# One more edge tile per turn by TensorE instead of GpSimd's gather, in each of two graph layers

## The reference

```python
h = jnp.maximum(_layernorm(x), 0.0)
# first layer
hw = h @ W0 + b0
agg = segment_sum(edge_weight[:, None] * hw[src], dst)
deg = segment_sum(edge_weight, dst)
x = x + relu(agg / (deg[:, None] + 1e-06))
h = jnp.maximum(_layernorm(x), 0.0)
# second layer
msg = gelu(concatenate([h[src], edge_attr]) @ W_msg + b_msg)
agg = segment_sum(msg, dst)
out = x + gelu(((1 + eps) * h + agg) @ W_upd + b_upd)
```

## Time and profile before

| | |
|---|---|
| median of 3 runs | 3535.41 us (3535.20 to 3536.32) |
| the profiled execution | 3536.93 us, span 3535.1 us |
| mean granted TensorE clock | 0.907 of full |
| PE, PEld busy | 82%, 78% of the span |
| POOL busy | 73%, 2,570.7 us |
| DVE, ACT busy | 61%, 55% |
| indirect DMAs (tiles gathered) | 1,323 in the first layer, 1,372 in the second |
| DMA engines | mean 62 GB/s |

### The profile page before, as it was taken

One profiled execution on the slowest core, in us unless ns is written; L12 is line 12 of the kernel. 1 busy time (PEld: TensorE's weight loads), 2 busy tenths in 40 slices (PEclk: granted clock), 3 DMA queues, 4 the chain that ended last, 5 costly groups with the idle time before them and its releaser, 6 DMA issues.

```text
span 3535.1 us, 89327 instructions
## 1 busy us (share of the span) xinstructions
PE 2887.9 (82%) x31003; PEld 2758.6 (78%) x31004; DVE 2160.5 (61%) x3525; ACT 1944.3 (55%) x6492; POOL 2570.7 (73%) x2720
## 2 busy tenths in 40 slices
PE   1988888887888888888778888888888888888887
PEld 1987877877877777778777878787787878787877
DVE  5766666666666666666655555556565655565653
ACT  3655565655555656555565555555454555555553
POOL 4777777777777777777457777777777777777774
PEclk9999999999899899999678989898988899898988
DMA  3322222222222222222123333333333333333331
GB/s 97 60 48 53 50 48 50 50 52 50 48 53 50 48 50 50 52 50 48 32 63 74 75 73 77 74 81 72 76 74 74 74 74 74 74 74 74 74 74 48
DMA packets 277341, 220.23 MB, mean 62 GB/s; under 512 B 81018, under 2 KB 208518, under 8 KB 277314
## 3 DMA queue, kind: packets, MB, share of 16 engines
q0 software_dynamic: 86240, 88.48, 16.6%
q1 hardware_dynamic: 191074, 131.40, 13.1%
HBM read 214.39 MB, written 5.30 MB: 62 GB/s over the span
## 4 chain that ended last, share of the span: by engine, by line
POOL 71%; issue 24%; SPq 2%; PE 1%; POOLq 1%; DMA 1%; ACT 1%; DVE 0%; DVEq 0%
POOL rows L436 71%; PE ps L719 1%; SPq L307 1%; SPq L328 0%; POOLq L434 0%; ACT sums_sb L566 0%; DMA h_table<-h_sb 0%; POOLq L427 0%; SPq L300 0%; DMA p_table<-h_sb 0%; PE ps L745 0%; PE ps L679 0%; DMA rows<-h_table,idx 0%; SPq L304 0%; DVE h_sb L834 0%
## 5 line engine op out<-in xcount | busy, mean ns | idle before, releaser
L647 PE MATMUL ps<-parts,pick_all 125*128 125x192 bf16 x19600 | 1767.9, 253 | 54.6 <-DVE pick_all L930 30.8
L930 DVE TENSOR_SCALAR pick_all<-src_bc,node_f 125x1280 bf16<-125x1280 int16 (+1 forms) x1960 | 1740.0, 953 | 71.1 <-issue 52.7
L647 PEld LDWEIGHTS ps<-parts,pick_all 125*128 125x128 bf16 x19600 | 1692.6, 101 | 87.5 <-issue 57.1
L436 POOL DMA_INDIRECT rows<-p_table,idx x1372 | 1295.6, 944 | 440.0 <-issue 440.0
L436 POOL DMA_INDIRECT rows<-h_table,idx x1323 | 1248.6, 944 | 415.9 <-issue 415.9
L511 ACT ACTIVATE onehot<-iota,dw 128x72 f32<-128x72 f32 x3136 | 809.3, 342 | 0.0
L679 PE MATMUL ps<-onehot,room 128*65 128x72 f32 (+1 forms) x6272 | 546.4, 248 | 268.9 <-ACT room L541 262.5
L679 PEld LDWEIGHTS ps<-onehot,room 128*65 128x65 f32 (+1 forms) x6272 | 488.4, 155 | 328.1 <-ACT room L541 293.5
L586 ACT ACTIVATE room<-room 128x512 f32<-128x512 f32 x196 | 123.6, 630 | 783.9 <-DVE room L1095 783.3
L1095 DVE TENSOR_TENSOR room<-ps,rows 128x512 f32<-128x512 f32 x196 | 135.5, 691 | 618.0 <-DMA rows<-p_table,idx 600.7
L769 PE MATMUL ps<-W1b_sb,eT 128*128 128x128 f32 x1568 | 259.7, 318 | 252.1 <-ACT eT L581 251.9
(11 more groups left out here) (87 smaller groups left out, 567.2 us busy)
## 6 DMA issues: line engine op xcount, KB each, us to landing
src_bc<-last_src SPq DMA_DIRECT2D x196, 312.5 KB
ea<-in_edge_attr_dram SPq DMA_DIRECT2D x196, 256.0 KB, 5.4
rows<-p_table,idx POOLq DMA_INDIRECT x1372
rows<-h_table,idx POOLq DMA_INDIRECT x1323
src_bc<-last_src SPq DMA_DIRECT2D x49, 156.2 KB
x_sb<-in_x_dram SPq DMA_DIRECT2D x5, 312.5 KB
h_table<-h_sb SPq DMA_DIRECT2D x5, 312.5 KB
p_table<-h_sb SPq DMA_DIRECT2D x5, 312.5 KB
```

The source lines that it names most:

```text
L436: nc.gpsimd.indirect_dma_start(out=rows[:, s, j, 0:D], out_offset=None, in_=table[:, :], in_offset=bass.IndirectOffsetOnAxis(ap=idx[:, s, ...
L647: last = nc.tensor.matmul(psG[(s + shift) % 2], pick[layer][(s + shift) // 2 % 2][0:PN, n, at:at + P], parts[:, n, :], start=(n == 0), sto ...
L930: last = nc.vector.tensor_scalar(pick[layer][i][0:PN, c * KN:(c + 1) * KN, :], src_bc[:, i, :, 0:w], node_f[:, c:c + 1], None, ALU.is_equal)
```

## The change

The extra tiles move from slot 2 of the first layer to the odd slots: 1 and 3 in the first layer (two for each body instead of one), and 1 in the second (one instead of none). `JP` becomes [7, 6, 7, 6] and [7, 6, 7, 7]. Three pairs in four (counted over the two layers) have a pick of three tiles now. The 50 matmuls of an extra tile are done in two halves of 25: the first half after the `gather` of the even group before it, the second before the `gather` of its own group.

In the second layer TensorE's `edge_product` of g+1 comes behind `windows` of g.

The table with target and weight numbers side by side (`dw_tab`, fp32) is split into `dst_tab` (int16) and `w_tab` (fp32); ScalarE copies both for a group in the first layer, and the target numbers alone in the second. Some one-time rows of the preparation now lie in the room of the pick buffer.

```diff
-    EXTRA = 2
-    JP = [[JG - (layer == 0 and s == EXTRA) for s in range(SLOTS)] for layer in range(2)]
+    EXTRA = ((1, 1), (1, 0))
+    JP = [[JG - (s % 2 == 1 and EXTRA[layer][s // 2]) for s in range(SLOTS)] for layer in range(2)]
...
-        dw_tab = sb("dw_tab", [P, NG, 2, J])
+        dst_tab = sb("dst_tab", [P, NG * J], i16)
+        w_tab = sb("w_tab", [P, NG * J])
...
+        def width(layer, i):
+            return PE3 if EXTRA[layer][i] else PE2
+        def extras(layer, b, i):
+            return b * sum(EXTRA[layer]) + sum(EXTRA[layer][0:i + 1])
...
# SyncE, load_bc
-                if layer == 0 and i == 0:
+                if EXTRA[layer][i]:
...
# ScalarE
-                nc.scalar.copy(dw[:, slot, :, :].rearrange("p q j -> p (q j)"),
-                               dw_tab[:, bass.ds(g, 1), :, :].rearrange("p a q j -> p (a q j)")).then_inc(s_dw[layer], 1)
+                if layer == 0:
+                    nc.scalar.copy(dw[:, slot, 1, :], w_tab[:, bass.ds(g * J, J)])
+                nc.scalar.copy(dw[:, slot, 0, :], dst_tab[:, bass.ds(g * J, J)]).then_inc(s_dw[layer], 1)
...
-                    if s == EXTRA:
-                        act.wait_ge(s_xrow, b + 1)
+                    if s % 2 and EXTRA[0][s // 2]:
+                        act.wait_ge(s_xrow[0], extras(0, b, s // 2))
...
# TensorE
+            def extra(layer, i, half):
+                for n in range(half * NK // 2, (half + 1) * NK // 2):
+                    last = nc.tensor.matmul(psX, pick[layer][i][0:PN, n, PE2:PE3], parts[:, n, :],
                                             start=(n == 0), stop=(n == NK - 1))
                 return last
+            def next_gathers(layer, b, s):
+                i = (s + 1) // 2 % 2
+                if s % 2:
+                    gather(layer, b, s, 1)
+                    if EXTRA[layer][i]:
+                        pe.wait_ge(s_xrow[layer], extras(layer, b + (s + 1) // SLOTS, i) - 1)
+                        extra(layer, i, 0)
+                else:
+                    if EXTRA[layer][i]:
+                        extra(layer, i, 1).then_inc(s_xpicked[layer], 1)
+                    gather(layer, b, s, 1)
...
             def second(b, last_body):
                 for s in range(SLOTS):
                     if not (last_body and s == SLOTS - 1):
                         edge_transpose(b, s, 1)
-                        gather(1, b, s, 1)
-                        edge_product(b, s, 1)
+                        next_gathers(1, b, s)
                     pe.wait_ge(s_msg, b * SLOTS + (s + 1 + 2))
                     windows(1, b, s, lambda j, s=s: msg[:, s % 2, j * D:(j + 1) * D], D)
+                    if not (last_body and s == SLOTS - 1):
+                        edge_product(b, s, 1)
...
# VectorE: the base of each group is taken off dst_tab (int16 in and out), padding is -20000
+            def extra_rows(layer, b, s):
+                dve.wait_ge(s_xpicked[layer], extras(layer, b, s // 2))
+                nc.vector.tensor_reduce(rows[:, s + 1, JG - 1, 0:D], psX.rearrange("p (q d) -> p d q", q=SPLIT),
+                                        AX.X, ALU.add).then_inc(s_xrow[layer], 1)
...
                     if not (last_body and s == SLOTS - 1):
+                        if s % 2 == 0 and EXTRA[1][s // 2]:
+                            extra_rows(1, b, s)
                         picked_rows(1, b, s, 1)
                         message_sum(b, s, 1)
```

More of the change, by code:

```diff
@@ L133, in two_layer_gnn @@
         src_bc = sb("src_bc", [PN, 2, KN, PE3 + 16], i16)
-        pick_all = sb("pick_all", [P, NK * (PE3 + PE2)], bf16)
-        pick = [[pick_all[:, 0:NK * w].rearrange("p (n e) -> p n e", n=NK),
-                 pick_all[:, NK * PE3:NK * (PE3 + PE2)].rearrange("p (n e) -> p n e", n=NK)] for w in (PE3, PE2)]
+        pick_all = sb("pick_all", [P, 2 * NK * PE3], bf16)
+        pick = [[pick_all[:, i * NK * PE3:i * NK * PE3 + NK * (PE3 if EXTRA[layer][i] else PE2)].rearrange(
+            "p (n e) -> p n e", n=NK) for i in range(2)] for layer in range(2)]
         flat_f = pick_all[:, :].bitcast(fp32)
@@ L496, in _ @@
                 high(0, u)
-            take(2, dw_tab[:, :, 0, :].rearrange("p g j -> p j g"), s_dwt)
+            take(2, dst_tab[:, :].rearrange("p (g j) -> p j g", j=J), s_dwt)
             for u in range(UNITS):
                 middle(0, u)
-            take(4, dw_tab[:, :, 1, :].rearrange("p g j -> p j g"), s_dwt)
+            take(4, w_tab[:, :].rearrange("p (g j) -> p j g", j=J), s_dwt)
             act.wait_ge(s_tables, 1)
@@ L649, in gather @@
                 last.then_inc(s_picked[layer], 1)
-            def extra(q):
-                for n in range(q * NK // 4, (q + 1) * NK // 4):
-                    last = nc.tensor.matmul(psX, pick[0][0][0:PN, n, PE2:PE3], parts[:, n, :],
+            def extra(layer, i, half):
+                for n in range(half * NK // 2, (half + 1) * NK // 2):
+                    last = nc.tensor.matmul(psX, pick[layer][i][0:PN, n, PE2:PE3], parts[:, n, :],
                                             start=(n == 0), stop=(n == NK - 1))
                 return last
[L658 to L669, removed]
+            def next_gathers(layer, b, s):
[9 more added lines that the diff above has]
+                    gather(layer, b, s, 1)
             def windows(layer, b, s, lhs, width):
@@ L694, in _ @@
             gather(0, 0, 0, 0)
-            extra(0)
-            extra(1).then_inc(s_xused, 1)
+            if EXTRA[0][0]:
+                extra(0, 0, 0)
             pe.wait_ge(s_tables, 1)
@@ L701, in first @@
                     if not (last_body and s == SLOTS - 1):
-                        gather(0, b, s, 1)
-                    next_extra(b, s, last_body)
+                        next_gathers(0, b, s)
                     pe.wait_ge(s_used[s], b + 2)
@@ L776, in _ @@
             gather(1, 0, 0, 0)
+            if EXTRA[1][0]:
+                extra(1, 0, 0)
             edge_product(0, 0, 0)
@@ L915, in onehots @@
                                         ALU.is_equal).then_inc(done, 1)
-            def width(layer, i):
-                return PE3 if layer == 0 and i == 0 else PE2
             def sources(layer, i, turn):
@@ L942, in next_pick @@
                     dve.wait_ge(s_pick[layer], 2 * b + (s + 3) // 2)
-                    if layer == 0 and s == 1:
-                        dve.wait_ge(s_xused, b + 1)
                     sources(layer, (s + 3) // 2 % 2, b + ((s + 3) // 4 + 1))
-                    last = pick_half(layer, (s + 3) // 2 % 2, 0)
-                    if layer == 0 and s == 1:
-                        last.then_inc(s_half, 1)
+                    pick_half(layer, (s + 3) // 2 % 2, 0)
                 else:
@@ L1021, in first @@
                     if not (last_body and s == SLOTS - 1):
+                        if s % 2 == 0 and EXTRA[0][s // 2]:
+                            extra_rows(0, b, s)
                         picked_rows(0, b, s, 1)
-                        if s == 1:
-                            extra_rows(b)
                     if last_body and s == 1:
@@ L1091, in message_sum @@
                 dve.wait_ge(s_em, g + 1)
-                dve.wait_ge(s_gat[slot], BODIES * 16 * JP[0][slot] + (b + (s + shift) // SLOTS + 1) * (16 * JG))
+                dve.wait_ge(s_gat[slot], BODIES * 16 * JP[0][slot] + (b + (s + shift) // SLOTS + 1) * (16 * JP[1][slot]))
                 dve.wait_ge(s_prow[1], g + 2)
+                if slot % 2 and EXTRA[1][slot // 2]:
+                    dve.wait_ge(s_xrow[1], extras(1, b, slot // 2))
                 dve.wait_ge(s_msg, g + 1)
```

25 lines of the change are left out of this document (10 added, 15 removed).

## The result

| | before | after |
|---|---|---|
| median | 3535.60 us (3535.20 to 3536.32, 4 runs) | 3414.22 us (3412.40 to 3414.84, 4 runs) |
| profiled execution, its span | 3536.9 us, 3535.1 us | 3412.4 us, 3410.6 us |
| granted clock, mean | 0.907 | 0.97 |
| first gather to last, first layer | 1650.5 us | 1590.2 us |
| last gather of the first to first of the second | 69.0 us | 67.5 us |

The ratio is 0.9653, 95% interval 0.9640 to 0.9667. The forecast was 3415, range 3406 to 3440. The two layers gave 60.4 and 61.3 us, the step between them 1.5 and the start 1.3 (first gather at 66.8 instead of 68.1 us).

What follows compares the result with a forecast made beforehand. GpSimd's number of gathers was taken as the bound, TensorE next. Profiled 3536.9 - 122.3 for gathers + 1.4 for layer ends = 3416.0; that execution being 1.5 us above the median, 3414.5, say 3415 us; range 3406 to 3440.

Steps and rivals of the forecast that it cites:

- Gathers: GpSimd, both layers: one gather fewer in each of 49 bodies, 61.1 and 61.2 us, together 122.3 us saved.
- TensorE's full-clock body: TensorE with the extra tile, without waits: 29.8 us against 32.4 in the first layer, 31.1 against 33.7 in the second.
- The slow-clock loss shrinks: TensorE's lower-clock work after waits: falls to 1 or 2 us a body, mean clock from 0.91 to 0.95 or more.
- Rival A: TensorE, both layers: lower clock after waits makes bodies 35.9 and 37.2 us; about 3756 us, 3459 with half the loss; 5%.
- The hand-over of the pick "just fits": VectorE to TensorE, second layer: pick ready some 6.6 us after the edge product, wanted 6.76 + 0.5 us after it.
- Rival B: Second layer: TensorE and VectorE hold each other up, 34.4 us a body instead of 33.7, +34 us, 3449 us; 8%.
- The order of the edge product costs and brings nothing: TensorE, second layer, edge product behind the one-hot product: between 1.2 us lost and 1.2 won a turn, taken as 0.
- Being late costs nothing: GpSimd's slot reuse: needed again some 24 us after issue, lateness eats from about 18 us; only mean body time counts.
- Start: Preparation: target-table writes add 3 to 6 us of ScalarE, covered by the first pick's broadcast wait until 77.42; cost 0.
- Ends: Ends of both layers: wider picks ahead of the last sums, last group sooner; bounds 0 and 3 us, 1.4 taken.
- "The chain still 94% GpSimd": Sign in the changed kernel's profile that the forecast is right: GpSimd still makes 94% of the chain of waits.
- Rival C: Only the first layer gains, the second being bound by TensorE at its old 34.9 us a body: 3476 us; 3%.

Runs made afterwards that it cites:

- the kernel with the gathers kept: Changed kernel with no gather left out (28 a body in both layers), the extra tiles' sums going to a spare tile: 3597.91 us, ratio 1.0169.
- the fill of 48: Changed kernel with 48 more picking-kind matmuls in each body of both layers, into a PSUM bank nobody reads: 3556.32 us, ratio 1.0055.
- all four pairs: Changed kernel with two extra tiles a body in the second layer too (26 gathers in both layers): 3505.51 us, ratio 0.9914.
- the fill of 24: Changed kernel with 24 more picking-kind matmuls in each body of both layers, into a PSUM bank nobody reads: 3413.33 us, ratio 0.9651.
- the kernels bound by TensorE: Changed kernel with 48 unread matmuls more in each body, 3556.32 us, and changed kernel with two extra tiles a body in both layers, 3505.51 us.
- the first layer alone: Changed kernel without the second layer's extra tile (28 gathers a body there, 26 in the first): 3481.68 us, ratio 0.9827.
- the four variants traced there: Changed kernel with second-layer extra tile removed, one extra tile per layer, two per layer, or old edge-product order: 5517.1, 5273.2, 5660.4, 5524.3 us.
- the third: Changed kernel with two extra tiles a body in both layers, on the chip where the kernel before took 5213.65 us: 5660.4 us.

## Why the prediction was right, step by step

- **Gathers: right.** Sum of the two terms 122.3 us, measured 60.4 + 61.3 = 121.7 from first to last gather. The 61.2 us of the kernel with the gathers kept is the same price in the other direction.
- **TensorE's full-clock body: right within 0.5 us,** 29.8 and 31.1 us against 29.3 and 31.4 with the fill of 48 and 31.4 from all four pairs. It is the number that decides. It came from two places of the trace before in which TensorE had nothing to wait for: one whole body in the first layer, but a single step of 6.76 us, taken four times, in the second. The free time there is 2.3 us and not 2.6.
- **The slow-clock loss shrinks: right in direction, and further than forecast.** 1 to 2 us a body were expected. In the second layer 33.7 - 31.4 - 1.7 leaves 0.6, and the ten slow rows of 50 matmuls, each 1.65 us too long, are 0.4 of it; in the first layer 32.4 - 29.3 - 1.8 leaves 1.3, of which 0.3 are short waits for issue. Rival A's cost (3 to 6 us a body at the lower clock) didn't come: a long wait was mostly followed by the lower clock in the first layer (16 of 17) and in 10 of 25 cases in the second, but with fewer such waits the mean clock rose from 0.93 and 0.90 to 0.98 and 0.99.
- **VectorE's body: right,** 25.5 and 24.2 us forecast, 1,147 / 44.7 = 25.7 and 1,115 / 46.6 = 23.9 measured.
- **The hand-over of the pick "just fits": wrong, without effect.** The row shows it missed by 2 us once in a body, not by a few tenths. The working asked when TensorE wants the pick if it is late; it was early, with 2.3 us to spare, and the wait is that spare time, as the fill of 24 shows. Rival B took the same wait for a loss.
- **The order of the edge product costs and brings nothing: right** (3413.13 and 3414.22).
- **Being late costs nothing: right within a layer,** since GpSimd's gathers wait for a buffer for only 1.2 us in all. As a general rule it lacks the layer's end, where the kernels bound by TensorE paid 19 to 24 us for it.
- **Start: right.** Four writes of the target table took 7.15 us in all, and the fp32 write behind them ended at 71.2 us:

```profile
52.93 7.15 ACT L487 CAST dst_tab<-ps 128x512 int16<-128x512 f32 x4 [8.50 <-PE ps L619]
...
68.20 2.96 ACT L487 COPY w_tab<-ps 128x512 f32<-128x512 f32 x4
...
76.37 4.57 DVE L938 TENSOR_SCALAR pick_all<-src_bc,node_f 125x1920 bf16<-125x1920 int16 x4 [7.22 <-DMA src_bc<-last_src]
```

  The first pick still waits for its broadcast and starts at 76.4, not after 77.5.
- **Ends: wrong sign.** +1.4 us were taken; the step between the layers lost 1.5 us, the start 1.3, the end 0.1. These 4.3 us, less the 0.6 that the layers gave too little, are the 3.6 by which the profiled execution (3412.4) lies below the sum (3416.0); what made these steps shorter was not looked into. That the forecast of the median is met to 0.8 us is partly luck. The forecast took 1.5 us off because the profiled execution before lay above its median, and the one after happened to lie 1.8 us below its own; together these hide nearly all of the 3.6.
- **"The chain still 94% GpSimd": wrong as a sign.** The page follows it back only to the start of the second layer, and gives

```profile
POOL 35%; issue 13%; PE 1%; ACT 1%; DVE 1%; POOLq 0%; DMA 0%; DVEq 0%
```

  Within the second layer's gathers it is GpSimd alone.

Rival C (only the first layer gains) is excluded by the pair of kernels: 61.5 us with the first layer alone, 121.4 with both.

## What to carry to other kernels

When one engine works through a fixed list, price the change as items removed times the cadence, and then ask only whether the next engine's body *at full clock* still fits; take that body from a stretch where it waits for nothing, since its waits and the slow clock behind them are slack that added work uses up first. A deep buffer hides lateness until the loop ends. Once the other engine is the bound, take its whole path through the loop, from its late start on: start plus bodies at its own length. Counting the bodies alone leaves out a late start (22 us here in the first layer), and adding the head start at the end to full bodies counts the same lateness twice. Stop at the tile that no longer fits (here the fourth pair cost 91 us where the third gave 61).

## What the runs showed of the hardware

- A gather (indirect DMA of 128 rows) on GpSimd took up to 1.60 us instead of 0.94 if it started more than 0.04 us into VectorE's 0.82 us subtraction of fp32 SBUF data, the longer the more of the subtraction was left, and kept its 0.94 if it had begun before (301 of 302); one-source compares on 2-byte data left it alone.
- A 128-column bf16 matmul with a new 125 x 128 weight each time took 0.057 us, a 192-column one 0.081 us: nearly in proportion to the columns.
- In the changed kernel a wait of TensorE of 2.0 us or more was followed by work at the lower clock in 16 cases of 17 in the first layer (waits of 2.0 to 2.4 us) and in 10 of 25 in the second (2.0 to 2.3 us); of the shorter ones two were, of 1.86 and 1.96 us.
- One chip ran the kernel before in 5214 us instead of 3536. In the four variants traced there TensorE waited again and again for "issue" between single matmuls (0.2 to 2.2 us in the third), while the gathers stayed at 944 to 947 ns. The reason is open.
